# Packed counts, an earlier restart at block boundaries, masks turned inside the node layer, and a reordered attention head

## The reference

```
m     = relu(relu([h[src], h[dst]] @ Wm1 + bm1) @ Wm2 + bm2)      # 1: message layer
m_sum = segment_sum(m, src);  u = h - softmax matching of the two halves
out   = relu(relu([h, m_sum, u] @ Wn1 + bn1) @ Wn2 + bn2)
e     = leaky_relu(al_s[src] + al_d[dst]);  alpha = segment softmax(e)   # 2: three attention
h'    = segment_sum(alpha * h[src], dst) + b                            #    layers of 4 heads
agg   = mean of the first 10 neighbours of every source row, or x if none;  agg @ W.T + b  # 3
z     = x + segment_sum(edge_weight * x[src], dst);  relu(z @ W1 + b1) @ W2 + b2            # 4
```

## Time and profile before

| | |
|---|---|
| median of 3 runs | 969.1 us |
| the profiled execution | 963.45 us |
| its span, first to last instruction | 961.5 us |
| mean granted TensorE clock | 0.984 of full |
| PE busy | 92% of the span |
| DVE, ACT, POOL busy | 69%, 52%, 31% |
| chain that ended last | PE 75%, DVE 13%, ACT 5%, issue 3% |
| pair loop | about 140 to 549 us |
| SKT, node layer, masks | about 549 to 606 us |
| attention layers | 610 to 706, 713 to 809, 815 to 911 us |

### The profile page before, as it was taken

The page is one execution under the profiler, slowest core; times in us unless marked ns, Lnnn a source line. Parts: engine busy times, 40 slices in busy tenths (PEclk is TensorE's granted clock), DMA queues, the critical chain, the costliest instruction groups (busy, mean ns, idle before and its releaser), DMA issues.

```text
span 961.5 us, 18681 instructions
## 1 busy us (share of the span) xinstructions
PE 881.2 (92%) x5491; PEld 547.6 (57%) x5526; DVE 665.9 (69%) x1778; ACT 502.8 (52%) x1009; POOL 298.3 (31%) x433
## 2 busy tenths in 40 slices
PE   8899959999899989998999988989998998899898
PEld 4657638878787878787878745422242222322244
DVE  6899966666666666666666764677767785967651
ACT  6421115555555656565555564666655665566621
POOL 8030075545454545454544400011132110112000
PEclk9999959999999999999999999999999999999999
DMA  3120041111211111111111300000000000000220
GB/s 83 47 66 1 0 154 55 44 66 44 66 44 66 44 66 44 66 44 66 44 60 44 70 2 1 1 1 1 1 1 0 1 1 0 1 1 0 86 90 22
DMA packets 19145, 35.87 MB, mean 37 GB/s; under 512 B 5280, under 2 KB 11552, under 8 KB 18976
## 3 DMA queue, kind: packets, MB, share of 16 engines
q0 software_dynamic: 7104, 19.41, 6.9%
q1 hardware_dynamic: 12000, 15.95, 4.9%
HBM read 29.56 MB, written 5.79 MB: 37 GB/s over the span
## 4 chain that ended last, share of the span: by engine, by line
PE 75%; DVE 13%; ACT 5%; issue 3%; DMA 1%; POOL 1%; DVEq 0%; ACTq 0%; POOLq 0%
PE PS L1420 9%; PE PS L1282 7%; PE PS L1276 6%; PE PS L1201 5%; PE PS L1405 5%; PE PS L1202 5%; PE PS L1149 5%; PE PS L1216 5%; PE PS L1411 4%; PE PS L1273 3%; PE PS L1323 3%; DVE OHd L998 3%; PE PS L1194 3%; PE PS L1374 2%; PE PS L1207 2%
## 5 line engine op out<-in xcount | busy, mean ns | idle before, releaser
L403 POOL DMA_INDIRECT BT<-Qtab,gidx x148 | 150.1, 1014 | 96.3 <-DVE gidx L825 61.1
L555 ACT ACTIVATE OHe<-OHs,sew 128x128 bf16<-128x128 bf16 x408 | 126.6, 389 | 62.1 <-PE PS L1282 61.6
L417 POOL TENSOR_SCALAR KV<-BT,pid 128x256 bf16<-128x256 uint8 x74 | 69.9, 945 | 175.0 <-DVE MS L900 169.5
L998 DVE CUSTOM_DVE_ANT_0 OHd<-PS,n1T 128x1024 bf16<-128x1024 f32 x96 | 112.1, 1220 | 9.5 <-PE PS L1374 9.5
L566 ACT ACTIVATE m2s<-m2s 128x512 f32<-128x512 f32 x68 | 42.8, 630 | 108.5 <-DVE m2s L926 108.5
L940 DVE TENSOR_SCALAR OHd<-iotaN,dstf 128x1024 bf16<-128x1024 f16 x136 | 63.9, 509 | 36.8 <-PE PS L1282 36.8
L926 DVE TENSOR_TENSOR m2s<-PS,bm 128x512 f32<-128x512 f32 x68 | 47.0, 691 | 54.1 <-PE PS L1202 54.1
L1201 PE MATMUL PS<-Wm,m1T 128*128 128x256 f32 x276 | 83.2, 384 | 0.0
L1202 PE MATMUL PS<-Wm,m1T 128*128 128x256 f32 x276 | 83.0, 383 | 0.0
L456 POOL TENSOR_TENSOR zl<-AL,Sx 128x8 f32<-128x8 f32 x12 | 2.6, 215 | 254.8 <-DVE Sx L998 254.8
L1282 PE MATMUL PS<-OHs,m2s 128*128 128x128 f32 x544 | 79.4, 290 | 0.0
(11 more groups left out here) (354 smaller groups left out, 1729.8 us busy)
## 6 DMA issues: line engine op xcount, KB each, us to landing
BT<-Wtab SPq DMA_DIRECT2D x1, 4096.0 KB, 12.8
BT<-Qtab,gidx POOLq DMA_INDIRECT x148, 2.8
BT<-Stab SPq DMA_DIRECT2D x1, 2048.0 KB, 10.4
Wtab<-H SPq DMA_DIRECT2D x4, 512.0 KB, 2.8
Wtab<-cs SPq DMA_DIRECT2D x4, 512.0 KB, 2.8
Qtab<-BT SPq DMA_DIRECT2D x1, 1024.0 KB, 4.5
Wn<-in_L_gnn_Wn SPq DMA_DIRECT2D x1, 1024.0 KB, 5.3
x<-in_x SPq DMA_DIRECT2D x1, 512.0 KB, 4.2
```

Of the source, the lines that this page charges most:

```text
L403: g.indirect_dma_start(out=G[:, p % SLOTS, k, :], out_offset=None, in_=Qtab, in_offset=bass.IndirectOffsetOnAxis(ap=gidx[:, p, k:k + 1], a ...
L555: a.activation(OHe[:, k, j, :], OHs[:, k, :], ACT.Copy, scale=sew[:, j, bass.ds(2 * g + k, 1)])
L998: v.tensor_tensor_reduce(junk[n % 2], bank(4, 2), mask[:, i, :], 1.0, 2 * FAR, ALU.subtract, ALU.max, Sx[:, i, hd:hd + 1]).then_inc(S("gat ...
```

## The change

1. **Counts leave in one instruction.** DVE multiplies banks 0 and 1 by 65536 on their way to a 32-bit integer tile `both` (on the memory of `BT`, where `LNC` will be). The high half of each word is the count (`CT`, int16 at a step of 4 bytes), the low half 64 times the kept count (`kept`). `SK`, the cast and the difference are gone. The transposes of L1306 read `kept`, ACT evicts them as int16 with another scale.
2. **The boundary.** ACT evicts the message sums before the weights. PE waits for the message sums alone, restarts bank 4 with the first rank matmul (start flag) instead of a zero matmul, then waits for weights (new wait `weights_out`) and counts and clears four banks; after the last block it clears none.
3. **The register load.** `span` and the values worked out of it are computed ahead of the wait for `ranks_read`.
4. **Masks in the node layer.** The transposes of CT stand between the eight groups of the first product, the masks on ACT too; `LNC` is made by columns after them. `n1T` and `mask` have a new buffer `room` of their own.
5. **Heads.** The distances of head 3 are made after the bound row of head 0. DVE, not POOL, makes the bound row of head 0; the eighth `greatest` comes after `s8`, `n8`, `s2`; ACT's first `ramp` comes before the bound row.
6. POOL clears `Apad` early.

```diff
@@ scalar
                 eng.wait_ge(S("ranks_done"), end + 1)
+                a.activation(msum[:, :, b * P:(b + 1) * P], ...).then_inc(S("msum_out"), 1)
                 if b >= 2:
                     eng.wait_ge(S(f"spilled{b % 2}"), 16 * (b // 2))
                 a.activation(TT[b % 2], bank(2, 2), ACT.Copy).then_inc(S("weights_out"), 1)
-                a.activation(msum[:, :, b * P:(b + 1) * P], ...).then_inc(S("msum_out"), 1)
...
+            eng.wait_ge(S("gathers_over"), 1)
+            eng.wait_ge(S("turned_onehots"), NASK)
             for i in range(8):
                 m, half = divmod(i, 2)
-                eng.wait_ge(S("lnc_counts"), i + 1)
-                a.activation(LNC[:, i, :], LNC[:, i, :], ACT.Ln).then_inc(S("lnc_logs"), 1)
                 eng.wait_ge(S("n1_done"), i + 1)
                 a.activation(n1T[:, m, half * BANK:(half + 1) * BANK], bank(6 + i % 2), ACT.Relu, ...)
-            eng.wait_ge(S("n2_done"), 1)
-            for i in range(NB):
                 eng.wait_ge(S("maskT_done"), i + 1)
                 a.activation(mask[:, i, :], bank(2 + i % 2).bitcast(i16), ACT.Relu, ...)
+                if i:
+                    logarithms(i - 1)
+            logarithms(NB - 1)
...
                 eng.wait_ge(S("banks_clear"), l + 1)
+                ramp(0, 1)
                 for hd in range(HEADS):
                     eng.wait_ge(S("rowT_done"), HEADS * l + hd + 1)
...
                     a.activation(rowA[:, hd % 2, :], bank(6 + hd % 2), ACT.Copy).then_inc(S("rowA_out"), 1)
+                    if hd == 0:
+                        distance_out(HEADS - 1, (1, 0))
@@ vector
                 eng.wait_ge(S("ranks_done"), end + 1)
-                v.tensor_copy(cntf[:], bank(0, 2)).then_inc(S("counts_out"), 1)
-                eng.wait_ge(S("counts_out"), b + 1)
-                v.tensor_copy(CT[:, b, :], cntf[:]).then_inc(S("ct_out"), 1)
-                eng.wait_ge(S("ct_out"), b + 1)
-                v.tensor_tensor(SK[:, b, :], cntf[:], CT[:, b, :], ALU.subtract).then_inc(S("kept_out"), 1)
-                eng.wait_ge(S("kept_out"), b + 1)
+                v.tensor_scalar(both[:, b, :], bank(0, 2), HALF, None, ALU.mult).then_inc(S("counts_out"), 1)
...
+            for i in range(NB + 1):
+                if i < NB:
+                    eng.wait_ge(S("maskT_done"), i + 1)
+                    if i >= 2:
+                        eng.wait_ge(S("lnc_ready"), i - 1)
+                    v.tensor_scalar(few(i), columns(CT, i), 0.5, FAR, ALU.is_lt, ALU.mult)...
+                    eng.wait_ge(S("lnc_shut"), i + 1)
+                    v.tensor_scalar(columns(LNC, i), columns(CT, i), 1.0, None, ALU.max)...
+                if i:
+                    eng.wait_ge(S("lnc_logs"), i)
+                    v.tensor_tensor(columns(LNC, i - 1), columns(LNC, i - 1), few(i - 1), ALU.add)...
...
-                for i in range(NB):
+                for i in range(NB - 1):
                     greatest(0, i)
...
                 eng.wait_ge(S("cols_ready"), l + 1)
+                greatest(0, NB - 1)
+                eng.wait_ge(S("gat_smax"), HEADS * NB * l + NB)
+                dcol = AL[:, :, HEADS]
+                link(v.tensor_tensor(zl[:, 0, :], dcol, Sx[:, :, 0], ALU.add))
+                link(v.scalar_tensor_tensor(lz[:, 0, :], zl[:, 0, :], SLOPE, zl[:, 0, :], ALU.mult, ALU.max))
+                link(v.tensor_tensor(Acol[:, 0, :], dcol, lz[:, 0, :], ALU.subtract))
...
+                for k in range(3):
+                    last = v.tensor_copy(Apart(k), halved(Acol[:, 0, :]))
+                    if k < 2:
+                        link(last)
+                        link(v.tensor_tensor(halved(Acol[:, 0, :]), halved(Acol[:, 0, :]), Apart(k), ALU.subtract))
+                last.then_inc(S("row_parts"), 1)
@@ tensor
-            for b in range(NB):
-                eng.wait_ge(S("src_onehots"), g0 + 1)
-                ranks(((0, beforeb, 0), (1, onesb, 0), (1, beforeb, 1))).then_inc(S("ranks_restarted"), 1)
+            eng.wait_ge(S("src_onehots"), 1)
+            restarted()
+            for b in range(NB):
                 with eng.Fori(g0, end) as g:
+                    eng.wait_ge(S("spans"), 1)
+                    span = eng.value_load(rngi[0:1, bass.ds(g, 1)], min_val=1, max_val=NB * NB * NB - 1)
+                    slot, first = eng.snap((g + 2) & (SLOTS - 1)), eng.snap((span >> 6) & (NB - 1))
+                    least, past = eng.snap((span >> 3) & 7), eng.snap((span & 7) + 1)
                     eng.wait_ge(S("ranks_read"), g + 1)
                     ranks(((0, notbefb, 0), (0, onesb, 1), (1, notbefb, 1))).then_inc(S("ranks_added"), 1)
-                    eng.wait_ge(S("spans"), 1)
-                    span = eng.value_load(rngi[0:1, bass.ds(g, 1)], min_val=1, max_val=NB * NB * NB - 1)
                     eng.wait_ge(S("turned_onehots"), g + 3)
-                    sources((g + 2) & (SLOTS - 1), (span >> 6) & (NB - 1))
+                    sources(slot, first)
                     eng.wait_ge(S("scaled_ready"), g + 1)
                     eng.wait_ge(S("counts_ready"), g + 1)
-                    with eng.Fori((span >> 3) & 7, (span & 7) + 1, 2) as d:
+                    with eng.Fori(least, past, 2) as d:
...
+                eng.wait_ge(S("msum_out"), b + 1)
+                if b + 1 < NB:
+                    restarted()
+                eng.wait_ge(S("weights_out"), b + 1)
                 eng.wait_ge(S("counts_out"), b + 1)
-                eng.wait_ge(S("msum_out"), b + 1)
-                for k in range(5):
-                    t.matmul(bank(k), zeros[:, 0:P], zeros[:, 0:BANK], start=True, stop=True)
+                if b + 1 < NB:
+                    for k in range(4):
+                        t.matmul(bank(k), zeros[:, 0:P], zeros[:, 0:BANK], start=True, stop=True)
...
+                if i == 0:
+                    eng.wait_ge(S("loops_added"), 1)
                 if i >= 2:
                     eng.wait_ge(S("mask_ready"), i - 1)
                 for j in range(NB):
                     last = t.transpose(bank(2 + i % 2).bitcast(bf16)[:, j * P:(j + 1) * P],
                                        CT[:, j, i * P:(i + 1) * P].bitcast(bf16), identb[:])
                 last.then_inc(S("maskT_done"), 1)
+            eng.wait_ge(S("n1_ready"), 8)
...
                     bound_row(hd)
+                    if hd == 0:
+                        distance_row(HEADS - 1)
+                    eng.wait_ge(S("rowA_out"), HEADS * l + hd + 1)
                     for j in range(NB):
                         bounded(hd, j)
+                        if hd == 0 and j == 1:
+                            eng.wait_ge(S("drow_out"), 2 * (HEADS * l + HEADS))
```

101 lines of the change are left out of this document (51 added, 50 removed).

## The result

The changed kernel took 920.2 us (median of 4 runs, 917.4 to 920.6), beside 969.75 for the kernel before: a ratio of 0.947, with an interval of 0.944 to 0.951. The profiled execution of after took 920.58 us, that of before 963.45: 42.9 us of difference between the two traces, where the sum said 34.8.

A forecast was written before the change was run, and what follows sets the result against it. PE was taken as the bound, its pair loop nearly all PE time, with waits mostly at block boundaries. Gains 15.1 + 13.8 + 2.0 + 2.2 + 1.7 = 34.8 us gave 928.6 profiled, 934.3 median; range 925 to 950.

The forecast's parts named there:

- Rival (b): Pair loop: the wait does not hold PE's sequencer, the 1.43 stays, pairs give 0; 953.7 us, chance 0.06.
- Rival (a): Pairs: register work does not pay, as DVE's ring or longer arithmetic keeps the gap; 948 us, chance 0.17.
- rival (d): Pairs: arithmetic ahead of the wait makes L1207 late in every pair; slower, 1002 us, chance 0.03.
- The pair term: Inside blocks: moved register work closes 0.23 of L1273's 0.31 us gap, 60 times: 13.8 us, bounds 0 and 18.6.
- the ring through DVE: Pairs: L1216 through message add and one-hots to the next L1273 takes 5.70 us, against 5.75 for PE alone.
- The boundary term: Seven block boundaries: L1282 comes at 197.9 instead of 200.09, a gain of 2.15 each, 15.1 us in all.
- The clock term: Pair loop: the two falls to half clock after boundary pauses disappear: 2.0 us, bounds 0 and 2.6.
- Rival (c): Layernorm 1: the clock falls after PE's idle matmuls end early, costing 5 us; 939 us, chance 0.10.
- The middle: Between pair loop and heads: -1.15 at the start, +3.5 for masks, -4.9 at the square root; gain 2.2 us.
- The heads: Attention heads, three times: PE adds its bounds at 631.6 instead of 632.15; 0.55 each, 1.7 us, bounds 0 and 4.
- The sign that I named for it: Head 0: the second L1411 group was to come some 5.2 us after the bound row.
- the 5.65 us: Whole kernel: the profiled 963.45 lies 5.65 under the median 969.1, a difference carried over to the forecast.

The follow-up runs named there:

- the registers alone: Kernel before, with only the load of `span` and its arithmetic moved ahead of the wait for the ranks: 929.1 us, ratio 0.961.
- the first kernel with the kept span: Kernel after, with the next pair's `span` loaded one pair ahead, before the transposes, into a lasting register: 916.8 us, ratio 0.948.
- faster level: Kernel after, unchanged, on chips where its pairs took 5.00 us: 912.5 and 912.7 us in its two repeat measurements.
- third trace of after: Profile of the kernel after, unchanged, from its second repeat on a further chip: 912.7 us, ratio 0.945.
- The experiment with two used loads: Kernel after, with a second load of `span` and its checks ahead of the wait for the ranks, both loads used: 942.6 us, ratio 0.971.
- the registers undone: Kernel after, with the load of `span` and the snaps put back behind the wait for the ranks: 949.2 us, ratio 0.982.
- first trace of after: Profile of the kernel after from the main measurement: median 920.2 us, profiled execution 920.58 us.
- in the second: Profile of the kernel after, unchanged, from its first repeat on a further chip: 912.5 us, ratio 0.944.
- The 0.42 us on DVE: Kernel after, with one more unused DVE operation ahead of the message addition in each pair: 912.9 us beside 912.7 for after.
- the two copies: Kernel after, with two unused copies of the counts on DVE behind the one instruction: 920.2 us, ratio 0.947.

## Why the prediction was right or wrong

**What was right.** The wait for `ranks_read` held PE's sequencer, and the load and its arithmetic behind it were the 1.43 of the earlier trace rows and the gap of 0.31 in the earlier trace rows. Rival (b), that the sequencer is not held, is out: the registers alone gave 39 us. The Trainium skill ("Perfetto Trace Analysis", Tensor Engine Instruction) speaks for that rival; these traces don't agree with it for this wait, whose threshold is in a register (whether that is the reason was not tested). In the first kernel with the kept span the sequencer's last step at the head of the loop began at 194.6, the rank was read at 195.37 + 0.08, and the next step began at 195.5. Rival (a) is out by the pairs of 5.00 to 5.05, and rival (d) by rank matmuls that start on time.

**The pair term was the failing step.** It said 13.8, with 18.6 as its upper bound, and measured 25.5, of which some 1.5 are the clock; so 24.0, or 0.40 a pair instead of 0.23. At the faster level the sixty pairs gain 30.6, and the miss is larger still. Two errors made it.

First, the ring through DVE, from L1216 over the message addition back to the top of the loop, which was to keep 0.08 of the gap of L1273. It keeps nothing of that gap: L1241 to L1300 is 0.60 in the median at both levels. I had worked out 5.70 us from an L1216 over DVE to the next L1273, against 5.75 for PE alone. In the third trace of after that way is 5.32 (2.19 to the end of the one-hots, 1.47 to the rank read, 1.44 to the sequencer's MOVE, and the 0.22 from there to L1273 that the kernel before shows), and PE alone needs 5.60. I had let the sequencer do the load and eleven steps after the ring's last event; in fact the load, its checks and one step stand ahead of the rank matmuls, they run beside DVE's own way to the rank read, and the sequencer is 1 us ahead of PE there.

Second, I looked only at the gap that the row of L1273 names. The inner loop had register stalls of its own that no "issue" of a grouped row shows: 1.11 for sixteen loads in the earlier trace rows, 0.95 at best, 16 x 0.056 + 0.05. The same lead takes them away. The experiment with two used loads brings back both pieces, at 0.64 us of register work, and so do the registers undone.

The ring itself was not imagined. In the first trace of after a pair takes 5.00 as long as the MOVE comes no later than 3.66 after the message sum, and 1.32 to 1.35 more than the MOVE in the 27 pairs where it comes later; and it comes late where the message addition does (3.55 with an addition at 4.63, 3.84 with one at 5.07). At the faster level the MOVE has about 0.1 us to spare, an estimate from 3.55 and 3.66. So the prediction was right that this way is about as long as PE's own; it looked for the cost at the wrong place and made it too large. What the ring did cost is 0.05 a pair in the median at the slower level, and next to nothing at the faster, where the MOVE comes that late in one pair of each of two traces.

**The boundary term was right in its mechanism and 3.8 us too large in this measurement.** It said 15.1 and measured 12.1, some 0.8 of it clock. I forecast 7.1 us from message sum to message sum; it was 7.7 on average. What I missed is a collision: the earlier load of `span` now falls into the store of 512 KB, and takes up to 1.15 us instead of 0.30. At the faster level it takes 0.54 to 0.80 and the boundary 7.15, and there the seven gain 16.1, or 15.3 without the clock. That this is so near to 15.1 is partly luck: the arithmetic was priced too high (one step stands ahead, not eight), and what decides there is not the sequencer but the rank read and the clearing matmuls, which I had expected earlier.

**The clock term** was right. The two falls of before cost about 0.5, 0.8 and 1.0 us in the pairs and the boundary that they touched, 2.3 in all, and no boundary of after fell to half clock. (With the registers alone one still did: a pair of 6.33 behind the third boundary, at a granted clock of 0.78.) Rival (c), a fall in layernorm 1, did not come in the first trace of after, but it came in seven of the fifteen traces of after and its variants. The granted clock from the start of the square root on, in the second and in the third trace of after:

```profile
556.00:560.00 4.00, 3.48 (x10) 1.32 (x11) 2.85 (x14) 3.23 (x7) 0.00 (x0) 0.62 0.00 0
```

```profile
555.00:559.00 4.00, 3.59 (x20) 2.03 (x21) 2.78 (x13) 3.42 (x8) 0.00 (x0) 1.00 0.00 0
```

Its price is 1.5 us (square root to the first maximum 8.06 instead of 6.55), not 5.

**The middle** said 2.2 and measured 2.8. The masks inside the first product cost 3.52 (3.5 forecast), the square root came 4.90 earlier (4.9). The way from the last message sum to the first product is 1.43 shorter, where I had 0.85 net; that is the 0.6.

**The heads** said 0.55 a layer and measured 0.95 to 1.0. The mechanism is the one described: PE waits for DVE at tile 2. DVE was done at 18.41 us after the first maximum instead of the 18.77 that I worked out, so the term is too small by 0.4 a layer, 1.2 in all. The sign that I named for it was worked out wrongly: the matmuls of tile 2 come 6.91 after the bound row, not 5.2, because the bound row moved by 2.1 and they by 0.95.

**What was in no term.** The part ahead of the loop took 0.4 more. And the 5.65 us between the profiled execution of before and its median did not carry over: after's profiled run of 920.58 lies at the top of its own runs. In the experiments single runs of before went from 962.3 to 973.0, so 963.45 was a quick execution of a kernel that spreads, and no constant of profiling. Against the profiled run the sum missed by 8.0 (10.2 from pairs, -3.8 from boundaries, 0.3, 0.6 and 1.2 from clock, middle and heads, -0.4 from the start, which is 8.1 by these rounded terms), against the median by 14.1.

## What to carry to other kernels

On PE a register load and its arithmetic belong ahead of a wait against a register's value, in the stretch where the sequencer only stands. What counts afterwards is the sequencer's lead over PE at each point of the loop: the same 0.37 us was free at one place and cost 0.13 and 0.23 at two others. Measure the lead in the sequencer's rows before placing anything.

An operation that is added to test a wait tests it only if the instruction behind it starts later. The 0.42 us on DVE filled an idle stretch and tested nothing, and the two copies were hidden by a longer wait elsewhere. Compare the start of the next instruction, not only the time of the kernel.

When a wait goes away, look at what the freed instruction now runs beside: here a load of 0.3 us met a store and cost 0.8 more. When two programs are compared within one per cent, run them on the same chip: one program took 912 and 920 us. And of two changes that meet at one wait, each can look worthless while the other holds it.

## What the hardware showed that was not expected

A register load from the on-chip memory by PE's sequencer took 0.30 us in every pair and 0.39 to 1.15 us beside a 512 KB store; with the store 2 us later no load in the loop took more than 0.318. A copy of 1024 16-bit counts at a step of 4 bytes from the on-chip memory took DVE 0.69, the eviction of as many from PSUM 1.21. The same program ran at pairs of 5.00 on three chips and of 5.05 in the first measurement, and variants of it at 5.08 to 5.09 on a fourth chip; there DVE and ACT started up to 0.45 us later behind the same matmuls, and why is open.
